# Delta rule chunks: the diagonal blocks of sixteen rows inverted by substitution on GpSimd through a DRAM scratch

## The chip, the core and the metric

The kernel runs on one core of one Trainium2 chip. The metric is the device time of one execution in microseconds (us). The engines are named as in the profile: PE is TensorE's matmul side, PEld its weight loads, DVE is VectorE, ACT is ScalarE, POOL is GpSimd, SP is the queue of SyncE, which here only starts DMAs and waits on semaphores.

## The reference, cut to what matters

The model is two layers over 2 x 1024 tokens of width 128: a gated delta rule, a stack of six local attention layers, a windowed attention and a mixture. The change touches the first only. Per head (2 sequences, 6 heads, key width 128, value width 32) it is a recurrence over the tokens:

```
S = S * exp(g_t)                      # S: 128 x 32
delta = (v_t - k_t S) * b_t
S = S + k_t (outer) delta ;  o_t = q_t S
```

The kernel doesn't step through the tokens. It takes chunks of 128 tokens: inside a chunk the deltas solve a triangular system (I + A) delta = rhs, where A is the strictly triangular 128 x 128 matrix of key products weighted by decay and b. So each chunk of each head needs the inverse of I + A (kept as `inv`) and its transpose (`invT`), and then only a few matmuls carry the state from chunk to chunk.

## The kernel before, in words

`delta_chunks` (L410 to L884) handles 16 units in turn: unit m is chunk m // 2 of sequence m % 2, all six heads at once, in two halves of three heads (a = 0, 1).

For a unit m the work is:

- `sums` (L822, POOL) and `decays` (L532, L534, PE), `decay_factors` (L695, ACT, an exp) and `gains` (L826, POOL) make the weights `gt`.
- `products` (L544, PE) multiplies keys with keys and queries, two heads at a time, into the one PSUM bank `g_ps`; `weigh` (L758, DVE) multiplies by `gt` into `amt`, which holds A transposed and the query part.
- `level` (L837, POOL) masks `amt` with the pattern of level l into `atm[l % 3]`. Level l joins diagonal blocks of 2^l rows to blocks of 2^(l+1).
- Level 0 needs no matmul: `first_turned` (L843, POOL), `first_turn` (L553, PE) and `first_inverse` (L763, DVE) write identity minus the masked matrix.
- Each level l = 1 to 6 then does, for both halves, `lower` (L566, for l = 6 L569; PE), `keep_lower` (L679, ACT), `left` (L591, for l = 6 L593; PE) and `change` (L771, for l = 6 L774; DVE). After each level but the last `turn_inverse` (L576, PE) and `keep_turned` (L683, ACT) renew the transpose.
- With the inverse done: `from_state` (L604), `turn_keys` (L521), `solve` (L612), `to_state` (L620, L621) on PE, `residual`, `solution`, `advance` on DVE, `fade_state` (L850) and `gated` (L856) on POOL.

The order on every engine is written out by hand, in a loop over slots s. In slot s unit s is inverted through levels 1 to 6; the recurrence of unit s - 1 and the preparation of unit s + 1 are put between the levels. Every engine works through its own list in order, and semaphores tie the lists together. A three-head step of fp32 matmuls (`lower`, `left`) is six instructions on PE, a three-head turn is three.

SP has three loads at the start of this stage and nothing after them. The stage is followed by `delta_outputs` (L887), after a barrier of all engines.

## Time and profile before

| | us |
|---|---|
| median of 3 runs (lowest, highest) | 3261.16 (3244.03, 3281.86) |
| the profiled execution | 3263.82 |
| its span, first to last instruction | 3262.1 |
| mean granted TensorE clock | 0.876 of full speed |
| PE busy over the span | 2885.2 (88%) |
| POOL busy over the span | 1830.5 (56%) |

The delta chunks take the stretch from about 195 us to 807 us of the span. What comes before is the projections and convolutions, what comes after is `delta_outputs`, then the local layers from about 880 us. In the profile a row of a stretch or of a group of instructions gives busy time and a count; busy time is not a wait, and PE's busy time has modelled ends. "[idle before <- releaser]" is how long an engine stood and what ended it.

### The profile page before, as it was taken

How to read it: one execution, taken by the hardware profiler on the slowest of the kernel's cores; microseconds unless marked ns; L12 is line 12 of the kernel's file. 1: busy time of each engine (PE TensorE's matmuls, PEld its weight loads, DVE VectorE, ACT ScalarE, POOL GpSimd, SP SyncE). 2: the span in 40 equal slices, each digit the busy share in tenths (PEclk: the TensorE clock that was granted, in tenths of full speed). 3: DMA queues.
4: the chain of work that ended last, by engine and by line, in shares of the span. 5: the costliest groups of instructions: out<-in, count | busy, mean ns of one | idle time of the engine just before them, and what ended most of it. 6: DMA issues, size and time to landing. Idle time of an engine off the chain costs nothing. (4 is left out here: it accounts for less than half of the span.)

```text
span 3262.1 us, 94066 instructions
## 1 busy us (share of the span) xinstructions
PE 2885.2 (88%) x38815; PEld 2010.7 (62%) x38815; DVE 1787.4 (55%) x3522; ACT 1542.9 (47%) x2863; POOL 1830.5 (56%) x2696
## 2 busy tenths in 40 slices
PE   5869999998588999999899999999899976999977
PEld 1259999998356666666566666666666653555444
DVE  5822222222276777776777777776777744434314
ACT  4722222223155656665666655666666641233223
POOL 0044444442188888887878888888878741111111
PEclk9968889887599999999999999999999997577677
DMA  1000000000211121212222121212111110000000
GB/s 29 0 6 1 1 1 1 1 1 17 94 39 49 43 62 41 82 41 64 57 57 63 41 73 50 60 53 74 41 41 48 41 31 13 1 1 1 1 11 14
DMA packets 60625, 109.93 MB, mean 34 GB/s; under 512 B 14366, under 2 KB 18734, under 8 KB 59438
## 3 DMA queue, kind: packets, MB, share of 16 engines
q1 hardware_dynamic: 59280, 102.69, 11.3%
q8 instruction: 310, 5.08, 0.6%
q10 hardware_dynamic: 926, 1.27, 0.1%
q14 instruction: 109, 0.89, 0.1%
HBM read 28.93 MB, written 1.05 MB: 9 GB/s over the span
## 5 line engine op out<-in xcount | busy, mean ns | idle before, releaser
L1681 POOL TENSOR_TENSOR l_rot_a<-l_rot_a,l_rot_b 128x512 f32<-128x512 f32 x384 | 483.8, 1275 | 113.5 <-DVE l_rot_b L1541 112.9
L1169 PE MATMUL l_A<-l_wts,l_H 128*128 128x512 f32 x768 | 416.0, 625 | 27.2 <-ACT l_H L1482 21.3
L1535 DVE TENSOR_TENSOR l_rot_a<-l_A,l_tab 128x512 f32<-128x512 f32 x384 | 265.0, 690 | 289.6 <-ACT l_sq L1401 278.2
L1690 POOL TENSOR_TENSOR l_qk<-l_rot_a,l_rn 128x512 f32<-128x512 f32 x384 | 388.7, 1044 | 21.5 <-POOLq L1728 21.2
L1401 ACT ACTIVATE l_sq<-l_A 128x512 f32<-128x512 f32 x384 | 230.9, 601 | 133.3 <-PE l_A L1169 129.0
L1407 ACT ACTIVATE l_pT<-l_T 128x512 f32<-128x512 f32 x192 | 109.0, 595 | 373.4 <-PE l_T L1215 372.9
L1541 DVE TENSOR_TENSOR l_rot_b<-l_A,l_tab 128x512 f32<-128x512 f32 x384 | 261.5, 681 | 0.0
L1545 DVE TENSOR_REDUCE l_ss<-l_sq 128x8 f32<-128x512 f32 x384 | 259.6, 676 | 0.0
L2010 ACT ACTIVATE a_pT<-a_t 128x384 f32<-128x384 f32 (+1 forms) x256 | 111.2, 463 | 261.2 <-PE a_t L1908 261.1
L1270 PE MATMUL l_T<-ident,l_qk 128*128 128x128 f32 x1536 | 212.6, 282 | 17.3 <-POOL l_qk L1690 14.6
L1270 PEld LDWEIGHTS l_T<-ident,l_qk 128*128 128x128 f32 x1536 | 177.8, 144 | 80.7 <-issue 54.9
L1908 PE MATMUL a_t<-a_qT,a_kT 32*128 32x384 f32 (+1 forms) x512 | 198.0, 651 | 28.3 <-ACT a_pT L2010 28.3
L1753 POOL TENSOR_TENSOR l_pn<-l_sd,l_rs 128x1024 f32<-128x1024 f32 x96 | 182.9, 1905 | 67.8 <-DVE l_rs L1563 67.8
L679 ACT ACTIVATE c_u<-c_ups 128x192 f32<-128x192 f32 x192 | 63.5, 330 | 304.6 <-PE c_ups L566 277.5
L771 DVE TENSOR_TENSOR c_inv<-c_inv,c_wps 128x192 f32<-128x192 f32 x160 | 56.7, 355 | 267.1 <-PE c_wps L591 266.6
L837 POOL TENSOR_TENSOR c_atm<-c_amt,c_blocks 128x768 f32<-128x768 f32 x96 | 156.2, 1642 | 81.6 <-DVE c_amt L758 78.4
L1244 PEld LDWEIGHTS l_O<-l_vw,l_pT 64*32 64x32 f32 x9216 | 135.9, 111 | 106.8 <-ACT l_pT L1407 89.3
L2042 DVE CUSTOM_DVE_ANT_0 a_junk<-a_s,a_mask 128x384 f32<-128x384 f32 (+1 forms) x256 | 125.7, 523 | 138.5 <-PE a_s L1897 136.7
L1276 PEld LDWEIGHTS l_T<-l_oT,l_wts 128*128 128x128 f32 x1536 | 186.4, 192 | 23.3 <-issue 11.3
L2107 POOL TENSOR_SCALAR_AFFINE_SELECT a_pT<-a_pT 128x512 f32<-128x512 f32 x56 | 35.7, 637 | 278.5 <-ACT a_pT L2010 278.5
L1276 PE MATMUL l_T<-l_oT,l_wts 128*128 128x128 f32 x1536 | 187.2, 275 | 0.7 <-ACT l_oT L1425 0.7
L1178 PE MATMUL l_O<-l_wts,l_H 128*128 128x512 f32 x384 | 183.9, 602 | 0.9 <-ACT l_oS L1418 0.5
(340 smaller groups left out, 6635.2 us busy)
## 6 DMA issues: line engine op xcount, KB each, us to landing
l_vw<-l_vn SPq DMA_DIRECT2D x384, 128.0 KB
l_vw<-l_vn SPq DMA_DIRECT2D x360, 64.0 KB
l_wts<-in_l_wts SPq DMA_DIRECT2D x18, 650.0 KB, 4.2
l_tab<-in_l_tables SPq DMA_DIRECT2D x6, 1024.0 KB, 5.2
l_wts<-in_l_wts SPq DMA_DIRECT2D x6, 635.5 KB, 4.1
result<-x SPq DMA_DIRECT2D x4, 256.0 KB, 2.3
d_w_qkv<-in_d_w_qkv SPq DMA_DIRECT2D x1, 864.0 KB
l_scales<-in_l_scales SPq DMA_DIRECT2D x6, 128.0 KB, 5.5
```

Of the source, the lines that this page charges most:

```text
L1169: pe.matmul(A[j % 2][:], cols(m), w_of(m)[:, C_QKV + 512 * j:C_QKV + 512 * j + 512], start=True, stop=True).then_inc(pq_done, 1)
L1178: pe.matmul(O[e][:], cols(m), w_of(m)[:, C_V + 512 * e:C_V + 512 * e + 512], start=True, stop=True).then_inc(v_done, 1)
L1270: last = pe.transpose(T[c % 2][:, P * i:P * i + P], qk[:, c, P * i:P * i + P], ident[:])
L1276: last = pe.matmul(T[0][:, 0:P], w_of(m)[:, C_WO + D * two:C_WO + D * two + D], oT[:, two, :], start=(two == 0), stop=(two == HP - 1))
L1401: act.activation(sq[:, j % 2, :], A[j % 2][:], ACT.Square).then_inc(sq_rdy, 1)
L1535: dve.tensor_tensor(rot_a[p][:, j, :].rearrange("p (a d) -> p a d", d=DH), src.rearrange("p (a d) -> p a d", d=DH), table[:, a, t:t + 1, : ...
L1541: dve.tensor_tensor(rot_b[:, j, :].rearrange("p (a e d) -> p a e d", a=8, e=2), swapped, sins.to_broadcast([P, 8, 2, DH // 2]), ALU.mult). ...
L1545: dve.tensor_reduce(ss[p][:, 8 * j:8 * j + 8], sq[:, j % 2, :].rearrange("p (a d) -> p a d", d=DH), AX, ALU.add).then_inc(ss_rdy, 1)
L1681: pool.tensor_tensor(rot_a[m % 2][:, j, :], rot_a[m % 2][:, j, :], rot_b[:, j, :], ALU.add).then_inc(rot_rdy, 1)
L1690: pool.tensor_tensor(qk[:, j, :].rearrange("p (a d) -> p a d", d=DH), rot_a[p][:, j, :].rearrange("p (a d) -> p a d", d=DH), rn[p][:, 8 * ...
L1753: pool.tensor_tensor(pn[:].rearrange("p a e k -> p e a k"), sd[m % 2][:].rearrange("p (e a) k -> p e a k", e=2), rs[:].rearrange("p (e a o ...
L1908: pe.matmul(t_ps[h % 2][:, c0:c1], kT[r, j, P * t:P * t + P], qT[r, j, around(t)], start=True, stop=True)\
```

## The change

Levels 0 to 3 of the doubling go. In their place the eight diagonal blocks of 16 x 16 of each of the six heads, 48 blocks in all, are inverted by forward substitution on POOL, with one block to a partition. The blocks get to that layout and back by way of DRAM: `amt` is written out in rows, the diagonal blocks are read into `bm` (48 partitions), the inverses `bx` are written back to the diagonal of a zeroed scratch matrix, and that matrix is read as `inv`. All four DMAs of a unit are issued on SP, each one waited for before the next that depends on it. Levels 4, 5 and 6 stay as they were. The transpose that level 4 needs is now a `turn_inverse(s, 3)` on PE. `amt` has three buffers in place of two. The slot order is rewritten: the decays are made two units ahead (slot s does unit s + 2), the products and the block inverse one unit ahead, and the loop has one more slot, starting at s = -2.

The core of the diff:

```diff
+FIRST, LAST = 4, LEVELS - 1
+BLK = 1 << FIRST
+PROBS = GH * P // BLK
...
-        blocks = sb("c_blocks", [P, LEVELS, P], BF16)
+        blocks = sb("c_blocks", [P, LAST - FIRST, P], BF16)
-        amt = [sb(f"c_amt{i}", [P, GH, 2, P]) for i in range(2)]
-        atm = [sb(f"c_atm{i}", [P, GH, P]) for i in range(3)]
+        amt = [sb(f"c_amt{i}", [P, GH, 2, P]) for i in range(3)]
+        atm = [sb(f"c_atm{i}", [P, GH, P]) for i in range(LAST - FIRST)]
+        eye = sb("c_eye", [PROBS, BLK, BLK])
+        bm = sb("c_bm", [PROBS, BLK, BLK])
+        bx = sb("c_bx", [PROBS, BLK, BLK])
+        bt = sb("c_bt", [PROBS, BLK, BLK])
+        lower_out = [nc.dram_tensor(f"c_lower_out{i}", (GH, P + 1, P), F32).ap() for i in range(2)]
+        first_in = [nc.dram_tensor(f"c_first_in{i}", (GH, P + 1, P), F32).ap() for i in range(2)]
...
+        def rows_of(matrix):
+            return bass.AP(tensor=matrix.tensor, offset=0, ap=[[P, P], [(P + 1) * P, GH], [1, P]])
+        def diagonal_of(matrix):
+            return bass.AP(tensor=matrix.tensor, offset=0, ap=[[BLK * (P + 1), PROBS], [P, BLK], [1, BLK]])
...
         def _(sp):
+            sp.wait_ge(cleared, 1)
+            for i in range(2):
+                sp.dma_start(rows_of(first_in[i]), inv[0][:]).then_inc(xo_done, 16)
+            sp.wait_ge(xo_done, 32)
+            for m in range(UNITS):
+                sp.wait_ge(amt_rdy, PAIRS * m + PAIRS)
+                if m >= 2:
+                    sp.wait_ge(bm_ld, 16 * (m - 1))
+                sp.dma_start(rows_of(lower_out[m % 2]), amt[m % 3][:, :, 0, :]).then_inc(ao_done, 16)
+                sp.wait_ge(ao_done, 16 * (m + 1))
+                if m >= 1:
+                    sp.wait_ge(bx_rdy, m)
+                sp.dma_start(bm[:], diagonal_of(lower_out[m % 2])).then_inc(bm_ld, 16)
+                sp.wait_ge(bx_rdy, m + 1)
+                if m >= 2:
+                    sp.wait_ge(inv_ld, 16 * (m - 1))
+                sp.dma_start(diagonal_of(first_in[m % 2]), bx[:]).then_inc(xo_done, 16)
+                sp.wait_ge(xo_done, 32 + 16 * (m + 1))
+                if m >= 2:
+                    sp.wait_ge(u_done, at_level(m - 2, LAST, 1))
+                    sp.wait_ge(tt_done, at_turn(m - 2, LAST - 1, 1))
+                sp.dma_start(inv[m % 2][:], rows_of(first_in[m % 2])).then_inc(inv_ld, 16)
...
             def decays(m, a):
                 pe.wait_ge(m1_rdy, m + 1)
                 if a == 1:
                     pe.wait_ge(gt_rdy, 2 * m + 1)
+                elif m >= 1:
+                    pe.wait_ge(amt_rdy, PAIRS * m)
...
             def turn_inverse(m, l, a):
-                pe.wait_ge(t_rdy, at_turn(m, l, a))
+                if l < FIRST:
+                    pe.wait_ge(inv_ld, 16 * (m + 1))
+                else:
+                    pe.wait_ge(t_rdy, at_change(m, l, a))
...
+            for s in range(-2, UNITS + 1):            # PE
+                for p in range(PAIRS):
+                    if has(s + 1):
+                        products(s + 1, p)
+                    if has(s - 1):
+                        from_state(s - 1, p)
+                if has(s + 2):
+                    decays(s + 2, 0)
+                for a in range(2):
+                    if has(s):
+                        turn_inverse(s, FIRST - 1, a)
+                if has(s + 2):
+                    decays(s + 2, 1)
+                for a in range(2):
+                    if has(s):
+                        lower(s, FIRST, a)
+                    if has(s - 1):
+                        turn_keys(s - 1, a)
+                for a in range(2):
+                    if has(s):
+                        left(s, FIRST, a)
+                    if has(s - 1):
+                        solve(s - 1, a)
...
+            for s in range(-2, UNITS + 1):            # ACT
+                if has(s + 2):
+                    decay_factors(s + 2, 0)
+                for a in range(2):
+                    if has(s):
+                        keep_turned(s, FIRST - 1, a)
+                if has(s + 2):
+                    decay_factors(s + 2, 1)
...
+            for s in range(-2, UNITS + 1):            # DVE
+                for p in range(PAIRS):
+                    if has(s + 1):
+                        weigh(s + 1, p)
+                if has(s - 1):
+                    residual(s - 1)
...
+            def block_inverse(m, lo, hi):
+                def step(ins, k):
+                    ins.then_inc(bx_step, 1)
+                    pool.wait_ge(bx_step, (2 * BLK - 1) * m + k)
+                if lo == 0:
+                    pool.wait_ge(bm_ld, 16 * (m + 1))
+                    if m >= 1:
+                        pool.wait_ge(xo_done, 32 + 16 * m)
+                    step(pool.tensor_copy(bx[:], eye[:]), 1)
+                for j in range(lo, hi):
+                    n, w = BLK - 1 - j, j + 1
+                    factor = bm[:, j, j + 1:BLK].rearrange("p (i o) -> p i o", o=1).to_broadcast([PROBS, n, w])
+                    step(pool.tensor_tensor(bt[:, 0:n, 0:w], factor, bx[:, j:j + 1, 0:w].to_broadcast([PROBS, n, w]), ALU.mult), 2 * j + 2)
+                    last = pool.tensor_tensor(bx[:, j + 1:BLK, 0:w], bx[:, j + 1:BLK, 0:w], bt[:, 0:n, 0:w], ALU.subtract)
+                    step(last, 2 * j + 3)
+                if hi == BLK - 1:
+                    pool.sem_inc(bx_rdy, 1)
...
+            for s in range(-2, UNITS + 1):            # POOL
+                if has(s - 1):
+                    fade_state(s - 1)
+                if has(s + 2):
+                    gains(s + 2)
+                if has(s + 3):
+                    sums(s + 3)
+                if has(s + 1):
+                    block_inverse(s + 1, 0, BLK - 1)
+                for l in range(FIRST, LAST):
+                    if has(s + 1):
+                        level(s + 1, l)
+                if has(s - 1):
+                    gated(s - 1)
```

## Rows read from the trace of the kernel before

**Rows 1.** The page's first part: busy time, share of the span, instructions.

```profile
PE 2885.2 (88%) x38815; PEld 2010.7 (62%) x38815; DVE 1787.4 (55%) x3522; ACT 1542.9 (47%) x2863; POOL 1830.5 (56%) x2696
```

**Rows 2.** Busy time by stretch: length, PE, PEld, DVE, ACT, POOL, granted clock, DMA.

```profile
270.00:774.00 504.00, 500.41 (x3642) 466.58 (x3641) 138.06 (x398) 148.35 (x356) 213.51 (x152) 0.86 0.00 1
```

**Rows 3.** One line's instructions, L826: shortest/median/longest ns, first and last start.

```profile
L826 POOL TENSOR_TENSOR c_gt<-c_gt,c_gain x16: 1469/1470/1472, 202.0 to 743.5; 128x768 f32<-128x768 f32 x16
```

**Rows 4.** Groups of weight loads by line, 270 to 774 us: busy, mean ns, idle.

```profile
L566 PEld LDWEIGHTS c_ups<-c_inv,c_atm 128*128 128x128 f32 x818 | 122.5, 221 | 5.1
L591 PEld LDWEIGHTS c_wps<-c_u,c_invT 128*128 128x128 f32 x826 | 119.4, 212 | 10.2 <-issue 4.6
L576 PEld LDWEIGHTS c_tps<-ident,c_inv 128*128 128x128 f32 x411 | 56.7, 177 | 1.9
```

**Rows 5.** Busy time by stretch, two stretches at the two clock levels.

```profile
413.00:434.00 21.00, 20.77 (x177) 19.38 (x175) 6.34 (x15) 6.55 (x17) 13.35 (x9) 0.99 0.01 2
433.00:447.00 14.00, 14.00 (x66) 12.97 (x66) 2.38 (x10) 3.45 (x8) 3.00 (x3) 0.52 0.00 0
```

**Rows 6.** PE and ACT in order of time: start, length, instruction, idle before.

```profile
196.69 1.49 PE L534 MATMUL c_gps<-c_m,c_tri 128*128 128x384 f32 x2
...
406.76 0.37 PEld L576 LDWEIGHTS c_tps<-ident,c_inv 128*128 128x128 f32 x3
...
407.37 0.81 PE L534 MATMUL c_gps<-c_m,c_tri 128*128 128x384 f32 x2
...
408.21 0.49 ACT L695 ACTIVATE c_gt<-c_gps 128x384 f32<-128x384 f32 x1 [0.32 <-PE c_gps L534]
...
443.45 0.66 PEld L576 LDWEIGHTS c_tps<-ident,c_inv 128*128 128x128 f32 x3
```

**Rows 7.** POOL in order of time, chained small operations of `rsqrt`.

```profile
20.31 0.22 POOL L71 TENSOR_TENSOR n_tmp<-n_tmp,n_mv 128x16 f32<-128x16 f32 x1 [0.18 <-POOL n_tmp L70]
...
173.36 0.59 POOL L71 TENSOR_TENSOR d_rs_tmp<-d_rs_tmp,d_ssq 128x192 f32<-128x192 f32 x1 [0.18 <-POOL d_rs_tmp L70]
```

**Rows 8.** Single lines' instructions on POOL: shortest/median/longest ns.

```profile
L71 POOL TENSOR_TENSOR m_etm<-m_etm,m_ess x3: 181/181/183, 3184.6 to 3187.6; 16x1 f32<-16x1 f32 x3
L1703 POOL COPY l_kT<-l_kT x36: 394/398/402, 941.7 to 2620.3; 128x256 f32<-128x256 f32 x36
L66 POOL TENSOR_SCALAR d_ssq<-d_ssq x1: 858/858/858, 170.2 to 170.2; 128x192 f32<-128x192 f32 x1
```

**Rows 9.** DMA issues: count, KB each, median us from issue to landing.

```profile
result<-x SPq DMA_DIRECT2D x4, 256.0 KB, 2.3
a_mask<-in_a_mask SPq DMA_DIRECT2D x1, 192.0 KB, 2.6
ident<-in_ident SPq DMA_DIRECT2D x1, 64.0 KB, 5.6
x<-in_x SPq DMA_DIRECT2D x1, 0.5 KB, 6.2
m_bcol<-in_m_bcol SPq DMA_DIRECT2D x1, 2.5 KB, 2.5
```

**Rows 10.** Groups of POOL by line, 270 to 774 us.

```profile
L837 POOL TENSOR_TENSOR c_atm<-c_amt,c_blocks 128x768 f32<-128x768 f32 x84 | 136.7, 1642 | 71.0 <-DVE c_amt L758 67.8 <-PE c_ups L566 3.2
L822 POOL TENSOR_TENSOR c_m<-c_tri,logdecay 128x768 f32<-128x768 f32 x13 | 19.1, 1471 | 0.0
L856 POOL TENSOR_TENSOR gate<-x,gate 128x192 f32<-128x192 f32 x14 | 8.3, 591 | 44.2 <-PE c_ups L566 31.9 <-DVE x L743 12.3
L850 POOL TENSOR_TENSOR c_state<-c_state,decay 128x192 f32<-128x192 f32 x14 | 7.1, 509 | 37.5 <-PE c_sps L604 37.5
```

**Rows 11.** In order of time: first unit's last `weigh`, last unit's `left`, last `gated`.

```profile
209.25 0.69 DVE L758 TENSOR_TENSOR c_amt<-c_gps,c_gt 128x512 f32<-128x512 f32 x1 [2.17 <-PE c_gps L544]
...
790.64 0.53 PE L593 MATMUL c_wps<-c_invT,c_u 64*64 64x64 f32 x6 [0.18 <-ACT c_invT L683]
...
806.90 0.59 POOL L856 TENSOR_TENSOR gate<-x,gate 128x192 f32<-128x192 f32 x1 [10.77 <-DVE x L743]
```

More of the change, by code:

```diff
@@ L537, in products @@
             def products(m, p):
-                if p == 0:
-                    pe.wait_ge(gt_rdy, 2 * m + 2)
+                if p == 0 and m >= 1:
+                    pe.wait_ge(bv_rdy, m)
+                elif p == 0:
+                    pe.wait_ge(gt_rdy, 2)
                 else:
@@ L620, in to_state @@
                     pe.matmul(s_ps[:, VD + HV * h:VD + HV * h + HV], kn[:, h, :], xd[:, h, :], start=True, stop=True, skip_group_check=True)
-                    mm = pe.matmul(s_ps[:, HV * h:HV * h + HV], amt[m % 2][:, h, 1, :], xs[:, h, :], start=True, stop=True,
+                    mm = pe.matmul(s_ps[:, HV * h:HV * h + HV], amt[m % 3][:, h, 1, :], xs[:, h, :], start=True, stop=True,
                                    skip_group_check=True)
                 mm.then_inc(od_done, 1)
-            def behind_lower(s, l, a):
-                if l == 1 and has(s - 1):
-                    from_state(s - 1, a)
-                if l == 2 and a == 0 and has(s - 1):
-                    turn_keys(s - 1, 1)
-                if l == 2 and a == 1 and has(s + 1):
-                    decays(s + 1, 0)
-                if l == 3 and a == 0 and has(s + 1):
-                    decays(s + 1, 1)
-                if l == 4 and a == 0 and has(s - 1):
-                    to_state(s - 1, 2)
-                if l == 4 and a == 1 and has(s + 1):
-                    products(s + 1, 0)
-                if l == 5 and a == 0 and has(s + 1):
-                    products(s + 1, 2)
-                if l == LAST and a == 1 and has(s + 1):
-                    first_turn(s + 1, 0)
@@ L643, in behind_left @@
-            def behind_left(s, l, a):
-                if l == 1 and a == 0 and has(s - 1):
-                    from_state(s - 1, 2)
-                if l == 1 and a == 0 and has(s + 1):
-                    turn_values(s + 1)
-                if l == 1 and a == 1 and has(s - 1):
-                    turn_keys(s - 1, 0)
-                if l == 2 and has(s - 1):
-                    solve(s - 1, a)
-                if l == 3 and has(s - 1):
-                    to_state(s - 1, a)
-                if l == 4 and a == 0 and has(s + 1):
-                    products(s + 1, 1)
-                if l == LAST and a == 0 and has(s + 1):
-                    first_turn(s + 1, 1)
@@ L659, in _ @@
-            pe.wait_ge(const_ld, 48)
-            pe.wait_ge(init, 1)
-            for s in range(-1, UNITS + 1):
-                for l in range(1, LEVELS):
-                    for a in range(2):
-                        if has(s):
-                            lower(s, l, a)
-                            if l >= 2:
-                                turn_inverse(s, l - 1, a)
-                        behind_lower(s, l, a)
-                    for a in range(2):
-                        if has(s):
-                            left(s, l, a)
-                        behind_left(s, l, a)
+            pe.wait_ge(const_ld, 64)
@@ new lines, in _ @@
+            pe.wait_ge(init, 1)
+            for s in range(-2, UNITS + 1):
[23 more added lines that the diff above has]
+                    if has(s):
+                        lower(s, FIRST + 1, a)
+                        turn_inverse(s, FIRST, a)
+                    if has(s - 1):
+                        to_state(s - 1, a)
+                for a in range(2):
+                    if has(s):
+                        left(s, FIRST + 1, a)
+                    if a == 0 and has(s - 1):
+                        to_state(s - 1, 2)
+                if has(s + 1):
+                    turn_values(s + 1)
+                for a in range(2):
+                    if has(s):
+                        lower(s, LAST, a)
+                        turn_inverse(s, FIRST + 1, a)
+                for a in range(2):
+                    if has(s):
+                        left(s, LAST, a)
```

175 lines of the change are left out of this document (67 added, 108 removed).

## The prediction

> **What bounds the kernel now.** I began with the page's busy shares: PE is the busiest engine over the whole span, POOL second among the others [rows 1]. A share over the whole span says little about one stage, so next the stretches. Between 270 and 774 us, fourteen units of the delta chunks, PE is busy 500 of 504 us and the weight loads alone 467, while POOL has 214, ACT 148, DVE 138 and DMA nothing [rows 2]. PE's modelled ends could flatter it, but the weight loads at 93% can't hide a wait for a chain: PE is truly full, and what leaves its list is time. The period of a unit is read from an instruction that occurs once in each: L826 starts at 202.0 the first time and 743.5 the sixteenth, 541.5 / 15 = 36.1 us [rows 3]. The stretch shows no DMA, so SP is free.
>
> By the code a unit has 266 instructions on PE: 72 for `lower`, 72 for `left`, 36 in the turns with `first_turn`, and 86 for the rest (2 + 6 + 6 + 12 + 24 + 12 + 24). The trace has 3642 in 504 us, 261 a unit; a few records are missing. The groups of levels dominate the loads [rows 4]. The clock moves between its two levels, 2.4 and 1.2 GHz: 177 instructions take 21 us at 0.99 (0.119 each), 66 take 14 us at 0.52 (0.212 each), and the stage as a whole has 0.86 [rows 2, 5].
>
> **PE's part.** Levels 1, 2 and 3 take away 6 `lower` and 6 `left` steps of 6 instructions and 3 turns of two halves with 3 each (turns 1 and 2 and the first turn; the turn of level 3 stays): 72 + 18 = 90 of 266, 34%. Read from the loads instead: 0.6 x (122.5 + 119.4) + 0.4 x 56.7 = 168 of 467, 36% even without the first turn [rows 2, 4]. So PE needs 176 / 266 x 36.1 = 23.9 us a unit at the clock of before. At the head of a slot products and `weigh` alternate on one bank, with `from_state` as cover; about 1 us for that and the two shortened last levels. PE's own bound: 25 us.
>
> **The new wait and its circle.** `turn_inverse(s, 3)` on PE now waits for the load of `inv`. Behind it in PE's list stand `decays(s + 2, 1)`, level 4 and the whole recurrence of unit s - 1. That decay feeds the exp on ACT, this feeds `gains(s + 2)` on POOL, and behind `gains` and `sums` in POOL's list stands the block inverse of unit s + 1, whose result makes the next load of `inv`. This is a closed circle once per slot, and I price it piece by piece.
>
> *Turn, decay, exp.* At the full clock a turn, its decay and the exp run from 406.76 to 408.70, 1.94 us, and the second turn adds 0.37: 2.3. At the low clock the turns are 0.66 each and the decay's fp32 matmuls 1.49 instead of 0.81: 3.6 [rows 6]. PE has just stood waiting there, so I take the upper one, 3.5.
>
> *Gains and sums.* 1.47 each [rows 3, 10]: 2.9.
>
> *Block inverse.* One copy of 256 elements and 30 dependent operations of n x w elements with n + w = 16. The products sum to 680 over 15 steps, 45 on average. A chained POOL operation of 16 elements takes 0.22, of 192 elements 0.59, each after a gap of 0.18 [rows 7]; the line through them gives 0.283 at 45, so 0.46 with the gap: 13.9, and 0.398 + 0.18 for the copy [rows 8]: 14.5 us. Lower end: 0.18 of work, as at one element, and the gap for all: 11.4. Upper end: each as long as 192 elements, 23.9, for no row has runs of 1 to 15 elements under a broadcast. I stay on the line because few partitions cost nothing extra (16 of them, one element: 0.181 [rows 8]) and `fade_state`, with a broadcast operand and 192 elements, takes 0.509 [rows 10], no more than the plain ones.
>
> *Two DMAs.* `bx` goes out to DRAM: 48 KB in runs of 64 B; the nearest row is the store of 256 KB in runs of 512 B, 2.3 us. The matrix comes in: 384 KB; the nearest row is `a_mask`, 192 KB in 2.6; with another half I take 3.1. With 0.15 before each, 5.7 us. Lower end 4.8 (2.3 and 2.5), upper end the two dearest landings, 5.6 and 6.2, which is 12.1 [rows 9].
>
> Here a rule speaks against the change: the runs of 64 B. The rows bound the store only by one with longer runs. The Trainium skill ("DMA: Bandwidth & Descriptors", the opening table) says that below 512 B the DMA engines read, modify and write and lose line rate. By that the store would take longer, perhaps by as much as it spends on its packets; as an estimate from that page, half a microsecond a unit, 8 us in all. No run here shows it, and the sum goes without it.
>
> Circle: 3.5 + 2.9 + 14.5 + 5.7 = 26.6, with handoffs 27 us. It is longer than PE's 25, so PE waits some 2 us a slot at the turn.
>
> **Not on the path, and what covers it.** The way out (`amt` to DRAM 2.8, blocks in 2.6, from the store and `m_bcol` [rows 9]) runs between `weigh(s + 1)` and the block inverse. SP can only issue it once the load of `inv` for unit s is under way, and then it lands some 3 us after that load; the block inverse starts 6.4 us after it. If PE reaches the head of the slot late this cover goes; then the path over two slots decides: rest of PE's slot 17, head 6, out and in 5.7, block 14.5, back 5.7, which is 49 for two, still under 27 each. POOL's remaining work (two masks 3.3 instead of six and a `first_turned`, `gated` 0.6, `fade_state` 0.5 [rows 10]) lies under the two DMAs; its total is 14.5 + 2.9 + 4.4 = 21.8 of 27. ACT and DVE lose ten and eight operations a unit and wait already. SP's queue carried nothing. The zeroing of the scratch (two stores of 2.3) lies before the first `weigh` ends.
>
> **The sum.** The first unit is weighed at 209.9 as before [rows 11]. The block inverse of unit 0 now stands behind `gains(1)`: two decays and exps at the low clock, some 2.4 each, 4.9, and `gains` and `sums`, 2.9: 217.8. Plus 14.5 and 5.7: `inv` of unit 0 is there at 238. Fifteen periods of 27 lead to 643. Slot 15 after its turn has 176 - 39 = 137 instructions less the decays, at 0.136 with a little waiting: 17, so 660. The last recurrence takes what it took, 791.1 to 807.5, 16.4 [rows 11]: 676.5. Before it was 807.5. That is 131 us less. The profiled execution took 3263.8, so 3133; it stands 2.7 above the median of the runs, and I predict 3132.
>
> **Rivals.**
>
> *PE stays the bound.* The block inverse goes at its lower end or the clock stays low; then a period is 25 and the time 3133 - 15 x 2 = 3103. For it: 27 and 25 are close. Against: the circle has four landings and gaps at favourable prices already. Chance 0.18.
>
> *The trips through DRAM are dear.* Upper landings in the circle, 12.1 instead of 5.7: period 33.4, and 3133 + 16 x 6.4 = 3235. For it: the only large load in short rows is x, 6.2. Against: that one moved 1 MB in all and `ident` stood behind it in the queue; the other three rows land in 2.3 to 2.6. Chance 0.10.
>
> *The steps on POOL are dear, and the kernel is slower.* The place is the 30 dependent operations; the price is that of the dearest small POOL operation, 0.858 with 0.19 of gap, 1.05 a step [rows 8]: 31 x 0.59 = 18 us more, period 45, time 3133 + 16 x 18 = 3421. The point from which it decides: 131 / 16 = 8.2 us more, that is 0.73 a step instead of 0.46. For it: shapes that no row has, and every one is on the path. Against: 0.858 was a first use; its successors were at 0.5 to 0.7 for four times the elements. Chance 0.09.
>
> *The clock falls.* PE waits in each slot. At 0.52 an instruction takes 0.212 instead of 0.136 [rows 5]: 176 make 37.3, period 37 and 3133 + 150 = 3283, no change. Against: PE would then be always busy, and with PE always busy the clock of before was 0.86 [rows 2]. The Trainium skill ("TensorE: Matmul & The Clock Gate", on what is happening) says that the low clock is the default and activity lifts it, so a wait each slot would favour this rival; the trace has low spells with PE full too [rows 5], so it neither bears this out nor speaks against it. Chance 0.06.
>
> **Numbers.** The forecast has 0.57. The four rivals make 1 with it. From 3085 (PE's bound with a clock slightly higher than before) to 3235 (dear DRAM trips) lie the forecast and the first two rivals, 0.85. One per cent is 33 us, about what a measurement of this kernel can tell from no change. Faster by more: 0.57 + 0.18 and a part of the dear trips, 0.78. Within: the rest of those and the clock, 0.13. Slower: 0.09.
>
> **What would show it.** POOL's steps should start every 0.4 to 0.55 us and a block inverse last 14 to 15; `gains` should start right after an exp whose decay waited behind the turn; the largest wait of PE should be the turn, released by the DMA of `inv`; L826 should recur every 27 us; the DMAs of a unit should land in 2 to 3.5. I am wrong if the steps take over 0.7, if POOL waits for `bm` and not for the exp, or if the clock of the stage is under 0.7.

## The result and the profile after

| | before | after |
|---|---|---|
| median (lowest, highest) of 4 and 4 runs, us | 3259.72 (3244.03, 3281.86) | 3102.51 (3071.02, 3110.8) |
| the profiled execution, us | 3263.82 | 3103.04 |
| its span, us | 3262.1 | 3101.3 |
| mean granted clock over the span | 0.876 | 0.873 |
| first `gains` to last `gated`, start, us | 202.0 to 806.9 [rows 3, 11] | 201.9 to 649.7 |

The ratio is 0.9495, with a 95% interval of 0.9409 to 0.9582. An execution more than 1.5% above the fastest of its kernel counts as slow and is left out of every ratio here, though not out of the medians. The forecast was 3132 in a range of 3085 to 3235. Of the 161 us between the two profiled executions 157 lie before the end of the delta chunks: their last `gated` comes that much earlier, and from there to the end it is 2455.2 us before and 2451.6 after.

In the code after, `gains` is L860, `sums` L856, the masks `level` L866, the block inverse L879 (copy), L883 (multiply) and L884 (subtract), `turn_inverse` L616, the decays L575 and L577, the exp L731, the products L589, `weigh` L799. The DMAs are L528 (`amt` out), L532 (blocks in), L536 (inverses out) and L541 (`inv` in).

The page after, its first part and two of its DMA rows, against [rows 1]:

```profile
PE 2707.9 (87%) x37375; PEld 1824.3 (59%) x37375; DVE 1738.0 (56%) x3395; ACT 1476.6 (48%) x2703; POOL 1833.4 (59%) x3112
...
c_lower_out<-c_amt SPq DMA_DIRECT2D x16, 384.0 KB, 2.5
c_inv<-c_first_in SPq DMA_DIRECT2D x16, 384.0 KB, 3.4
```

PE has exactly 38815 - 37375 = 1440 instructions less, 90 for each of 16 units. The same stretches as [rows 2, 5] of before, now of the changed kernel (columns as there, with GB/s at the end):

```profile
410.00:433.00 23.00, 22.73 (x179) 20.32 (x178) 6.92 (x21) 6.67 (x16) 15.63 (x37) 1.00 0.18 42
215.00:560.00 345.00, 328.12 (x2256) 287.73 (x2257) 89.65 (x266) 86.89 (x206) 216.59 (x514) 0.85 0.15 36
270.00:590.00 320.00, 317.39 (x2241) 281.90 (x2241) 88.92 (x270) 85.13 (x202) 194.56 (x463) 0.88 0.16 37
```

In the steady part PE is busy 317 of 320 us. The engine that bounded the stage before bounds it still, which the forecast denied. 2241 instructions in 320 us make 25.1 us for a unit of 176, and the period read from `gains` says the same; this is its row, to be laid beside [rows 3]:

```profile
L860 POOL TENSOR_TENSOR c_gt<-c_gt,c_gain x16: 1469/1470/1472, 201.9 to 566.2; 128x768 f32<-128x768 f32 x16
```

The second of the sixteen starts at 214.90, so fourteen periods take 351.3 us, 25.1 each. That mean is made of two kinds of slot: ten take 22.6 to 23.4 us, and four, each with a stretch of some 20 us at the low clock, take 29.6 to 31.4. The waits for the load of `inv`, from the view of the one line L616 (its lengths in ns, then what ended PE's idle time before it, in us, and how often; PE and its weight loads counted apart):

```profile
L616 PE MATMUL c_tps<-ident,c_inv x288: 272/273/476, 234.5 to 631.1; 128*128 128x128 f32 x144
its engine sat idle before it (us, times) until:
  DMA c_inv<-c_first_in: 32.9, 9
```

This is 33 us on the two sides of PE together, 17.2 of it at the first unit. The forecast had a wait of 2 us in every slot. Now one slot at the full clock in order of time (start, length, instruction, idle time before it), read as the circle was priced:

```profile
405.65 0.32 SPq L536 DMA_DIRECT2D c_first_in<-c_bx  x1
...
405.84 1.13 PE L589 MATMUL c_gps<-kqT 128*128 128x256 f32 x4
...
407.63 0.38 SPq L541 DMA_DIRECT2D c_inv<-c_first_in  x1
...
411.84 0.81 PE L577 MATMUL c_gps<-c_m,c_tri 128*128 128x384 f32 x2
...
412.48 0.82 PE L616 MATMUL c_tps<-ident,c_inv 128*128 128x128 f32 x6
...
413.48 0.81 PE L577 MATMUL c_gps<-c_m,c_tri 128*128 128x384 f32 x2
...
414.32 0.49 ACT L731 ACTIVATE c_gt<-c_gps 128x384 f32<-128x384 f32 x1 [0.38 <-PE c_gps L577]
...
414.89 1.47 POOL L860 TENSOR_TENSOR c_gt<-c_gt,c_gain 128x768 f32<-128x768 f32 x1 [2.68 <-ACT c_gt L731]
...
416.32 1.47 POOL L856 TENSOR_TENSOR c_m<-c_tri,logdecay 128x768 f32<-128x768 f32 x1
...
417.73 0.39 POOL L879 COPY c_bx<-c_eye 48x256 f32<-48x256 f32 x1
...
428.36 0.21 POOL L884 TENSOR_TENSOR c_bx<-c_bx,c_bt 48x15 f32<-48x15 f32 x1
...
428.47 1.13 PE L589 MATMUL c_gps<-kqT 128*128 128x256 f32 x4
428.65 0.32 SPq L536 DMA_DIRECT2D c_first_in<-c_bx  x1
...
430.62 0.38 SPq L541 DMA_DIRECT2D c_inv<-c_first_in  x1
...
435.11 0.82 PE L616 MATMUL c_tps<-ident,c_inv 128*128 128x128 f32 x6
```

Everything the forecast drew is there: the exp behind the second decay behind the turn, `gains` right after it, the block inverse behind `sums`, the two DMAs. But the block inverse takes 10.84 us (417.73 to 428.57), not 14.5. The load issued at 407.63 lands 3.4 later, at about 411.0, and PE comes to the turn at about 412.2. The circle at the full clock is 2.3 + 0.1 + 2.9 + 10.85 + 0.1 + 2.0 + 3.4 = 21.7; PE's own list takes 22.6 (L589, 405.84 to 428.47). It is a near miss: the circle has about 1 us of slack. The way out has little too: the blocks are read at 414.11 and land 2.1 later, at 416.2, and the block inverse starts at 417.73.

### The profile page after: what moved, and what is told of

Its sections match the earlier page's. It is cut to its first block and busy times, and to the rows that moved or that the text cites. A ratio compares the mean times of both kernels' runs of the same rounds, so it can differ in the third digit from the quotient of the medians.

```text
span 3101.3 us, 91235 instructions
## 1 busy us (share of the span) xinstructions
PE 2707.9 (87%) x37375; PEld 1824.3 (59%) x37375; DVE 1738.0 (56%) x3395; ACT 1476.6 (48%) x2703; POOL 1833.4 (59%) x3112
## 3 DMA queue, kind: packets, MB, share of 16 engines
q1 hardware_dynamic: 111808, 117.52, 13.8%
## 5 line engine op out<-in xcount | busy, mean ns | idle before, releaser
L1207 PE MATMUL l_A<-l_wts,l_H 128*128 128x512 f32 x768 | 416.1, 626 | 25.5 <-ACT l_H L1520 21.5
L1946 PE MATMUL a_t<-a_qT,a_kT 32*128 32x384 f32 (+1 forms) x512 | 197.9, 650 | 28.3 <-ACT a_pT L2048 28.2
L1314 PEld LDWEIGHTS l_T<-l_oT,l_wts 128*128 128x128 f32 x1536 | 186.3, 192 | 23.5 <-issue 11.3
L1282 PE MATMUL l_O<-l_vw,l_pT 64*32 64x64 f32 x9216 | 156.9, 237 | 13.8 <-issue 11.2
L1207 PEld LDWEIGHTS l_A<-l_wts,l_H 128*128 128x128 f32 x768 | 127.6, 200 | 65.8 <-issue 38.9
L1253 PE MATMUL l_T<-ident,l_pn 128*128 128x128 f32 x768 | 125.0, 301 | 45.3 <-DVE l_H L1607 44.9
```

The source lines that it names most:

```text
L1207: pe.matmul(A[j % 2][:], cols(m), w_of(m)[:, C_QKV + 512 * j:C_QKV + 512 * j + 512], start=True, stop=True).then_inc(pq_done, 1)
L1282: last = pe.matmul(O[e][WIN * wd:WIN * wd + WIN, DH * pair:DH * pair + DH], pT[r, pair, WIN * wd:WIN * wd + WIN], keys, start=True, stop=True,
L1314: last = pe.matmul(T[0][:, 0:P], w_of(m)[:, C_WO + D * two:C_WO + D * two + D], oT[:, two, :], start=(two == 0), stop=(two == HP - 1))
L1946: pe.matmul(t_ps[h % 2][:, c0:c1], kT[r, j, P * t:P * t + P], qT[r, j, around(t)], start=True, stop=True)\
```

## The experiments

Three theories. **P**: PE's list is the bound, the circle is hidden. **C**: the circle is the bound, or so near to it that PE's gain can't be had without it. **K**: PE is the bound, but its time is instructions times the granted clock, and what is done to the stage moves the clock; it was formed only after "less work on PE" had been run. All medians are set against the kernel before on the same chips. In the tables, "last `gains`" and "last `gated`" are start times in the profiled execution and "clock" is the mean from 215 to 560 us.

### The changed kernel again, for comparison

> The changed kernel itself once more, as the common base of the others. Its trace shows a unit every 25.1 us on average (22.6 in stretches at the full clock), PE busy 317 of 320 us, and the circle turn, exp, gains, sums, block inverse, two DMAs at about 21.7 us at the full clock. Theory P (PE is the bound, the circle has about a microsecond of slack): 3100, within 1%. Theory C (the circle sets the period, PE only fills it): the same time; this run tells nothing apart, the next three are read against it.

3074.79 us (3071.45 to 3094.29), ratio 0.945 [0.9416, 0.9484]; last `gains` 555.7, last `gated` 629.9, clock 0.87. The same program as above; the profiled executions differ by 32 us in all and 20 us in the stage. Eleven of its fourteen periods take 22.6 to 23.4 us, three 30.4 to 30.8. The intervals of the two ratios overlap, so below it is this second run that experiments are compared with (by the ratios where the chip is another), and a difference under some 25 us is not read as one.

### No substitution: the circle cut by 10 us

```diff
-                    pool.wait_ge(bx_step, (2 * BLK - 1) * m + k)
+                    pool.wait_ge(bx_step, m + k)
...
-                for j in range(lo, hi):
+                pool.wait_ge(bx_step, m + 1)
+                for j in range(0):
```

The 30 dependent operations are left out, so the identity goes through the scratch in place of the inverses; copy and DMAs stay.

> The 30 dependent POOL operations of each block inverse are left out (the copy of the identity stays, and all four DMAs), so the circle is 10.4 us shorter and PE has the same work. Theory P: only the first unit, before PE has anything to do, gets 10.4 us shorter, and the few waits at the turn go: 10 to 25 us less than the changed kernel, near 3083. Theory C: every period shrinks until PE's own work stops it, so clearly more, 60 us or above.

3079.03 us (3042.47 to 3089.4), ratio 0.9415 [0.9368, 0.9462]. No wait on the load of `inv` is left:

```profile
L616 PE MATMUL c_tps<-ident,c_inv x288: 272/273/473, 224.8 to 616.8; 128*128 128x128 f32 x144
its engine sat idle before it (us, times) until:
  issue: 4.1, 17
```

Taking 30 x 0.35 = 10 us out of each turn of the circle, 160 us of POOL's work, changes nothing in the total that the measurement can tell: the ratio's interval overlaps the changed kernel's. P had 10 to 25 us less, and that isn't shown either. The periods in the profiled executions tell more than the total. From the fourth `gains` on they are the same with and without the substitution, 22.6 to 22.9 us at the full clock and 30.4 to 30.8 in a slot with a low spell. Only at the head of the stage, before PE's list is full, are two of them shorter, 15.1 and 18.2 us for 23.4 and 23.2. The last `gains` starts at 535.0 (555.7 in the changed kernel), but the last `gated` at 635.3 (629.9): from 545.7 on the clock stays low to the end of the stage, and what the head won is lost there. The circle is not the bound, and C in its strong form falls.

### Less work on PE

```diff
-                for k in range(HALF):
+                for k in range(HALF if l == LAST or m == 0 else 1):
```

The same edit stands in `lower` and in `left`. In levels 4 and 5 (from unit 1 on) they compute one head of three: 32 of 176 instructions of a unit go, and part of the computation with them. A second kernel has both edits, this one and the missing substitution.

> In levels 4 and 5 only one head of three is multiplied in lower and left (all three in unit 0), so PE has 32 of 176 instructions less in each unit; POOL, DMAs and the other engines keep theirs. Theory P: the period falls until the circle stops it, from 25.1 to about 22.5 to 23, so 30 to 40 us less than the changed kernel, and PE now waits at the turn for the load of inv in nearly every slot. Theory C: no change, within 8 us.

> Both at once: 32 PE instructions less per unit and the 30 POOL operations left out. Theory P: the circle no longer stops PE, which gives back its whole 32 x 0.14 = 4.5 us a unit, 65 to 70 us, and 10 in the first unit: 75 to 85 us less than the changed kernel. Theory C: the same as without the substitution alone, since then the circle's gain is what counts, with some of PE's added.

| | median us | ratio, 95% | last `gains` | last `gated` | clock |
|---|---|---|---|---|---|
| changed | 3074.79 | 0.945 [0.9416, 0.9484] | 555.7 | 629.9 | 0.87 |
| less PE | 3136.4 | 0.9628 [0.9598, 0.9658] | 596.8 | 679.3 | 0.68 |
| less PE, no substitution | 3121.43 | 0.9567 [0.9537, 0.9597] | 585.0 | 669.9 | 0.68 |

Neither P nor C allows this: less work, and 62 us more time. With the circle cut it is 47 us more, so the circle isn't the reason. (Cutting it gives this kernel some 15 us, and the two ratios' intervals don't overlap; 13 of them are two shorter periods at the head of the stage.) What moved is the clock, from 0.87 to 0.68, with PE still busy nearly all the time. The median turn on PE takes 418 ns instead of 273, and nine of the fourteen periods of the first of the two kernels take 27.4 us. This brought up K; in the prediction a lower clock stood only as a rival tied to waits.

### Is it the clock? PE work added back

```diff
+                for i in range(1 if l == LAST else 1):
+                    pe.matmul(u_ps[a][:, 192:448].rearrange('p (h t) -> p h t', h=2), identb[:], blocks[:], start=True, stop=True, skip_group_check=True)
```

The kernel with less PE work, with matmuls added whose results nobody reads: one of 256 bf16 columns ahead of each half of `lower` and `left` in levels 4, 5 and 6, two of 128 columns for each pair in `to_state` and in `from_state`. In the kernel below it ("wide fillers") the computation is whole, and only the last level's and `to_state`'s ten are added: the line above reads `range(1 if l == LAST else 0)` there.

> The kernel with two heads of three left out of lower and left in levels 4 and 5 (3136 us at a clock of 0.68 in the stage) with fillers: a 256-column bf16 matmul ahead of each half of lower and left in all three levels, two of 128 columns in each to_state and one pair in from_state. PE gets more work than in that kernel. Theory K: the clock of the stage goes back above 0.85 and the time falls by 40 us or more, to 3070 to 3095. Theory W (that kernel was slower through some wait, not the clock): the time stays or goes up by 15.

> Nothing is left out; ten bf16 matmuls per unit are added whose result nobody reads: one of 256 columns ahead of each half of lower and left of the last level, two of 128 columns in each to_state, the narrow stretch of a slot (64 and 32 columns) in which the spells at 1.2 GHz began. They cost PE about 0.8 us a unit at the full clock. Theory K (the time is PE's list at the clock that it is granted, and the narrow stretch loses the clock): the three spells of 20 us between 240 and 600 us go or get short, 25 us back for 13 spent, so 5 to 25 us less than the changed kernel. Theory P without the clock: 13 us more.

The stretch from 240 to 540 us of the kernel with less PE work, then of the same with the fillers, then of the whole computation with ten fillers, then of the changed kernel:

```profile
240.00:540.00 300.00, 286.47 (x1553) 245.16 (x1551) 74.17 (x225) 72.49 (x175) 168.44 (x405) 0.69 0.14 33
```

```profile
240.00:540.00 300.00, 286.31 (x2300) 241.24 (x2299) 94.93 (x288) 89.15 (x220) 213.46 (x512) 0.99 0.18 43
```

```profile
240.00:540.00 300.00, 295.38 (x2332) 259.81 (x2332) 88.02 (x267) 83.87 (x201) 198.70 (x474) 1.00 0.16 39
```

```profile
240.00:540.00 300.00, 294.03 (x2101) 260.83 (x2101) 82.92 (x252) 80.98 (x192) 189.53 (x450) 0.89 0.15 37
```

The first two show K for this kernel. PE is busy the same 286 us in both, but 1553 instructions get through in one and 2300 in the other. The kernel with the added matmuls does strictly more and takes 3040.48 us (3035.54 to 3045.81), ratio 0.9327 [0.9276, 0.9377], against 3136.4: 96 us less, 98 by the ratios, and more than the 40 or so that K had asked for. Its last `gains` starts at 516.8 and its last `gated` at 583.9, instead of 596.8 and 679.3. The Trainium skill ("TensorE: Matmul & The Clock Gate", on what is happening) has activity lift the clock from its low default; these two agree in direction, 0.69 to 0.99, though the busy share of PE is the same in both.

The same kernel measures the circle. With the clock held and PE's list shorter, its turn waits for `inv` again and again:

```profile
L618 PE MATMUL c_tps<-ident,c_inv x288: 272/273/477, 232.2 to 569.0; 128*128 128x128 f32 x144
its engine sat idle before it (us, times) until:
  DMA c_inv<-c_first_in: 32.6, 19
```

Much of the 32.6 us is the first unit's wait, but from the fifth `gains` on every period is 21.5 or 21.6 us. Here the circle is the bound, and it takes what adding up its pieces gave, 21.7.

For the whole computation the fillers do less good: clock 0.97 in the stage, and the mean period is 23.5 us (last `gains` 540.9) where the comparison run has 24.5 (last `gains` 555.7). At the full clock a period is 23.6 instead of 22.6, so the ten fillers cost 1 us a unit. But the median is 3100.41 us (3084.0 to 3123.07), ratio 0.9518 [0.947, 0.9566]. From 581.0 on, where the last units run out, the clock stays low for 109 us, 47 of them inside the stage, and the last `gated` starts at 627.5, only 2 us before that of the comparison run: what the stage won by its middle it lost at its end. The profiled execution, 3084.0 us, is the shortest of the six, so this trace doesn't show what the others spent more. The kernel isn't faster than the changed one.

### Fillers to the end, and in the kernel before

```diff
-                for i in range(1 if l == LAST else 0):
+                for i in range((l == LAST) + (m >= UNITS - 2)):
...
+                for i in range(2 * (m >= UNITS - 3)):
+                    pe.matmul(s_ps[:, 2 * VD:512], identb[:], causal[:], start=True, stop=True, skip_group_check=True)
...
-                for i in range(2):
+                for i in range(2 + 2 * (m >= UNITS - 3)):
```

This is set against "wide fillers". The last units get more of them. The kernel before gets the same ten as "wide fillers".

> Nothing is left out. The ten wide matmuls of before, and in the last three slots, which lack the products and decays of later units, more of them: one of 256 columns ahead of each half of lower and left in every level of units 14 and 15, two more of 128 columns in to_state and two in from_state of units 13 to 15. With the ten alone the stage had the full clock until 581 us and then 1.2 GHz to its end at 627. Theory K (PE's list at the granted clock): the last slots keep the full clock and end some 15 to 20 us earlier, so the last gating at about 610 and 5 to 20 us less than the changed kernel. If the clock falls at the end for another reason, 2 us more than with the ten.

> The kernel of before with the same ten wide matmuls per unit in the last level and in to_state (nothing left out). Its stage had a granted clock of 0.86 and 36.1 us a unit, with a spell at 1.2 GHz in each unit. Theory K: if the fillers hold the clock, a unit takes 36.1 x (1 - 0.14) + 0.8 = 31.9 and the kernel 60 us less; if they miss the stretch where the spells begin (the start of the next slot, levels 1 and 2), the clock stays and it takes 10 us more. In the first case more than a third of what the change brought could have been had without it.

To the end: 3086.2 us (3066.56 to 3099.44), ratio 0.9451 [0.9407, 0.9495], level with the changed kernel's 0.945; K's 5 to 20 us less are not shown. This time spells of the low clock came at 365 and 539 us in the middle of the stage (20.5 us each), and the end had the full clock until 624.5 but for a spell from 601 to 607.5: last `gains` 560.6, last `gated` 636.2, clock 0.91. So the same fillers (up to unit 13 the two kernels are the same) that had 1.00 from 240 to 540 in one execution don't hold it in another; whether fillers can give a gain in the whole computation stays open.

In the kernel before: 3264.48 us (3256.61 to 3288.93), ratio 1.0012 [0.9981, 1.0043]. The stretch of [rows 2], of before with fillers:

```profile
270.00:774.00 504.00, 499.84 (x3699) 462.77 (x3698) 137.12 (x388) 145.21 (x349) 208.80 (x149) 0.87 0.00 1
```

Clock 0.87 for 0.86, about one low spell in each unit as before. The fillers bring nothing where they don't move the clock. Their cost is under what the ratio can tell; in the profiled execution a period is (753.9 - 200.9) / 15 = 36.9 us for 36.1.

### A longer circle

```diff
...
+                    for r in range(2):
+                        step(pool.tensor_tensor(bt[:, 0:n, 0:w], factor, bx[:, j:j + 1, 0:w].to_broadcast([PROBS, n, w]), ALU.mult), 3 * j + 2 + r)
...
```

Each multiply of the substitution is done twice: 15 operations, 5.1 us, more in the circle and none on PE.

> Each multiplication of the block inverse is done twice (15 more dependent POOL operations, 0.34 us each with the gap, 5.1 us a unit); nothing is left out. The circle grows from 21.7 to 26.8 us at the full clock. Theory P (PE's list is the bound at 22.6 at the full clock, the circle has one microsecond of slack): 5 in the first unit, and about 1.5 to 4 in each period, in all 35 to 65 us more than the changed kernel. Theory C (circle sets the period now): 16 x 5.1 = 82 us more. Theory K (what counts is the clock of the stage): PE now waits in every slot, so the clock of the stage falls under 0.8 and the time goes up by more than 82.

3178.65 us (3166.05 to 3187.65), ratio 0.9738 [0.9683, 0.9794]: 104 us more than the changed kernel in its run, 94 by the ratios. Last `gains` 632.9, last `gated` 731.5, clock 0.78, and now PE does stand at the turn:

```profile
L616 PE MATMUL c_tps<-ident,c_inv x288: 272/417/477, 239.4 to 712.9; 128*128 128x128 f32 x144
its engine sat idle before it (us, times) until:
  DMA c_inv<-c_first_in: 117.1, 20
```

The period is (632.9 - 214.8) / 14 = 29.9 us. At the full clock the circle would be 21.7 + 5.1 = 26.8, but eight of the fourteen periods are 28.2 to 28.4, and that is what this circle takes. In the slot shown PE waits 5 us, the granted clock goes to its low level within that wait (324.2 to 331.0), and turn, decay and exp behind it take 3.7 us (327.19 to 330.86) and not 2.3:

```profile
327.19 1.54 PE L616 MATMUL c_tps<-ident,c_inv 128*128 128x128 f32 x6 [5.03 <-DMA c_inv<-c_first_in]
...
330.37 0.49 ACT L731 ACTIVATE c_gt<-c_gps 128x384 f32<-128x384 f32 x1 [1.11 <-PE c_gps L577]
```

The load of `inv` lands in 3.7 us, 0.3 later than in the changed kernel, with the store of `amt` now issued right behind it. The six other periods, 29.2 to 40.2, hold longer low spells. So this is the forecast's mechanism at work, one step to the side of the change, and here its 3.5 for turn and exp behind a wait comes out. The price, 94 to 104 us, is far above 16 x (26.8 - 25.1) = 27 us and above P's 35 to 65. It doesn't tell C's 82 from K's "more than 82", but the clock is under the 0.8 that K named.

### An extra semaphore increment in each step

```diff
...
                     pool.wait_ge(bx_step, (2 * BLK - 1) * m + k)
+                    pool.sem_inc(bx_tick, 1)
```

The steps of `rsqrt` from which the forecast took the gap of 0.18 increment a second semaphore after each operation, with an instruction of its own (`sem_inc`); the substitution doesn't. Here it does.

> Each step of the block inverse adds one to a further semaphore after its wait, as rsqrt does; nothing else changes. The chained operations of rsqrt stood 0.18 us apart, those of the block inverse 0.08. If the extra increment is the difference, the gap goes to 0.18 and the block inverse from 10.8 to 13.9 us; if not, the gap stays at 0.08.

POOL in order of time, the changed kernel, then this one:

```profile
400.07 0.29 POOL L883 TENSOR_TENSOR c_bt<-c_bm,c_bx 48x64 f32<-48x64 f32 x1
400.44 0.31 POOL L884 TENSOR_TENSOR c_bx<-c_bx,c_bt 48x64 f32<-48x64 f32 x1
400.83 0.30 POOL L883 TENSOR_TENSOR c_bt<-c_bm,c_bx 48x63 f32<-48x63 f32 x1
```

```profile
400.20 0.29 POOL L884 TENSOR_TENSOR c_bt<-c_bm,c_bx 48x64 f32<-48x64 f32 x1 [0.18 <-POOL c_bx L885]
400.67 0.31 POOL L885 TENSOR_TENSOR c_bx<-c_bx,c_bt 48x64 f32<-48x64 f32 x1 [0.18 <-POOL c_bt L884]
401.16 0.29 POOL L884 TENSOR_TENSOR c_bt<-c_bm,c_bx 48x63 f32<-48x63 f32 x1 [0.18 <-POOL c_bx L885]
```

The lengths are equal, 0.29 and 0.31. Only the gap differs: 400.07 + 0.29 to 400.44 is 0.08, against 0.18. So the missing 0.10 of each step is this second increment, issued as its own instruction. One execution, 3146.19 us; a block inverse takes 13.8 us (418.31 to 432.10), PE waits at the turn in 22 places (78.3 us on its two sides together), the clock is 0.79 and the last `gated` starts at 692.3, 43 us later than in the first profile of the changed kernel and 62 later than in the second. Ten of the fourteen periods are 24.6 to 26.5 us, above the 22.6 of PE's list: with the gap that the forecast took, the circle is the bound, as it said.

### Dense blocks in DRAM

```diff
-                sp.dma_start(bm[:], diagonal_of(lower_out[m % 2])).then_inc(bm_ld, 16)
+                sp.dma_start(bm[:], bass.AP(tensor=lower_out[m % 2].tensor, offset=0, ap=[[BLK * BLK, PROBS], [BLK, BLK], [1, BLK]])).then_inc(bm_ld, 16)
...
```

`bm` is read and `bx` written as whole blocks of 1 KB in place of 16 runs of 64 B, from and to the head of the scratch; the values are then not those of the diagonal blocks.

> The blocks are stored to and read from one dense piece of DRAM in place of the diagonal of the matrix (same bytes, 1 KB in a row for each partition where it was runs of 64 B with gaps); the values that the levels then use aren't the inverses. In the changed kernel the store lands in 2.0 us and the read in 2.1. If runs of 64 B cost extra, both land earlier, at 1.5 or less; if the landing is all fixed cost, both stay within 0.2.

One execution, 3106.3 us, last `gated` 655.5. The DMAs from 230 to 560 us, of the changed kernel and then of this one (last figure: us from issue to landing):

```profile
c_bm<-c_lower_out SPq DMA_DIRECT2D x13, 48.0 KB, 2.1
c_first_in<-c_bx SPq DMA_DIRECT2D x13, 48.0 KB, 2.0
```

```profile
c_bm<-c_lower_out SPq DMA_DIRECT2D x14, 48.0 KB, 1.7
c_first_in<-c_bx SPq DMA_DIRECT2D x13, 48.0 KB, 1.6
```

The runs of 64 B cost 0.4 us a transfer (0.3 for the read if the comparison run is taken, where it lands in 2.0), between the two outcomes that were expected. The Trainium skill ("DMA: Bandwidth & Descriptors", the opening table) has transfers below 512 B lose line rate, and the trace agrees in direction. It gives no time for it: the half microsecond was the prediction's own estimate, and it came near. The circle isn't the bound in this kernel, so the gain isn't expected at the end; one execution can't show more.

### The transpose by DMA

```diff
+                sp.dma_start(diagonal_of(turned_in[m % 2]), bxT[:]).then_inc(xoT_done, 16)
...
+                sp.dma_start(invT[m % 2][:], rows_of(turned_in[m % 2])).then_inc(invT_ld, 16)
...
+                    pool.tensor_copy(bxT[:], bx[:].rearrange("p i j -> p j i")).then_inc(bxT_rdy, 1)
```

A version that takes more from PE: `invT` at level 3 comes through a second scratch, so six transposes of PE and two copies of ACT go; with the fillers to the end. The computation is whole.

> Nothing is left out. The transpose that level 4 needs is no longer made by PE: POOL copies the blocks transposed, SP stores them to a second scratch and loads invT from it, so PE has 6 instructions and ACT 2 less per unit, and the decays no longer stand behind the load of inv; fillers as in the kernel with fillers to the end. Theory P with the clock held: 0.8 us a unit less than that kernel, 13 us in all. Against it: the two further DMAs share the queue, and the load of invT lands 1 to 2 us after that of inv; if the circle decides, no gain or up to 20 us more.

3075.93 us (3050.85 to 3107.63), ratio 0.9406 [0.9362, 0.945]; last `gains` 534.1, last `gated` 622.5, clock 0.96:

```profile
240.00:540.00 300.00, 294.38 (x2325) 261.15 (x2325) 89.34 (x271) 77.23 (x183) 211.77 (x505) 0.99 0.24 59
```

Its periods are 22.8 to 23.5 us, it has no low spell between 261 and 571 us, and from 571.8 on the clock is low. It is the shortest stage of all whole versions and has the lowest ratio of them, but the interval overlaps the changed kernel's. No version with the whole computation was shown to be faster than the change itself.

## Why the prediction was right or wrong, point by point

**The total** was right in direction and inside the range; 30 us too slow. Its last step is a slip: 3133 less 2.7 is 3130, not 3132. **The mechanism was not the forecast's but its first rival's**, PE stays the bound, with 0.18 of chance and 3103 us; measured 3102.5. The fit of that figure is luck in part, since the changed kernel's own executions go from 3071 to 3111.

**PE's part** held: 90 instructions a unit are gone, to the instruction, and a unit takes 25.1 us where 25 stood, as a mean of slots of 22.6 and of some 30. The reasoning "PE is truly full, what leaves its list is time" gave the result. But it holds only at a given clock, as the kernel with less PE work shows: there PE was just as full, and what left its list was not time.

**The circle** was drawn rightly and priced wrongly, at 27 where it takes 21.7, and 21.5 where it was made the bound. The failed step is the gap in the block inverse:

| term, us | forecast | measured at the full clock |
|---|---|---|
| turn, decay, exp | 3.5 | 2.3 |
| `gains`, `sums` | 2.9 | 2.9 |
| block inverse | 14.5 | 10.84 |
| two DMAs | 5.7 | 2.0 + 3.4, and 0.1 |

The line through the lengths [rows 7] held: 0.283 at 45 elements forecast, 0.26 and 0.28 the medians of L883 and L884. Short runs, the broadcast and 48 partitions cost nothing that shows: 15 elements take 0.21, where the row with 16 had 0.22. The gap of 0.18 came from rows of operations that are followed by a second semaphore increment. The trace of before has chained operations without one as well, in the local layers, and they would have given the right price. POOL in order of time, kernel before:

```profile
917.58 0.26 POOL L1725 TENSOR_TENSOR l_rn_t<-l_rn_t,l_ss 128x36 f32<-128x36 f32 x1
917.93 0.31 POOL L1726 TENSOR_SCALAR l_rn_t<-l_rn_t 128x36 f32<-128x36 f32 x1
918.33 0.26 POOL L1727 TENSOR_TENSOR l_rn<-l_rn_t,l_rn 128x36 f32<-128x36 f32 x1
```

From 917.58 + 0.26 to 917.93 is 0.09. With 0.08 the sum is 30 x (0.283 + 0.08) + 0.48 = 11.4, just where the forecast's lower end was, and the circle 23.9, or 22.7 with the 2.3 of the full clock: under PE's 25. The other term that was too high, 3.5 for turn and exp, rested on "PE has just stood waiting there", which follows from the circle being the bound; it fell with it. Where PE does wait, in the kernel with the longer circle, it is 3.7.

**The DMAs** were near. The load of 384 KB takes 3.4 where 3.1 stood, the store with runs of 64 B 2.0 where 2.3 stood, the way out 2.5 and 2.1 where 2.8 and 2.6 stood. Landings like the two dearest of [rows 9], 5.6 and 6.2, never came (the longest of the four kinds is 4.6, of `inv` 3.9), which takes the dear trips away as a rival. The half microsecond for runs of 64 B, which the sum left out, was 0.4, and the measured 2.0 includes it.

**What was said to lie off the path** did: the way out, POOL's masks, SP's queue. Between 260 and 620 us POOL stood ahead of the block inverse once, for 4.1 us, and not for `bm`. But the way out has 1.5 us of cover in the slot shown, not the 3.4 of the forecast (6.4 less 3), since SP issues `amt` only when `weigh` is done, at 411.56, after the load of `inv` has landed.

**The sum** went: first `inv` at 234.5 (238 forecast), the last unit's first turn at 606.7 (643), fifteen periods of 24.8; the end of the stage at 650.3 (676.5). The last slots took 43.6 us where 17 + 16.4 stood, and they ran at the low clock:

```profile
600.00:650.00 50.00, 44.25 (x228) 42.30 (x228) 7.71 (x30) 6.89 (x16) 6.70 (x12) 0.54 0.04 9
```

So 36 us less up to the last turn and 10 more behind it leave the stage 26 us under the forecast.

**The rivals.** Dear steps on POOL and dear trips through DRAM did not come: 0.35 a step, 2.0 to 3.4 a trip. The clock did not fall in the change, 0.88 in the steady stretch against 0.86, but the rival named the sharpest danger. It was tied to waits of PE and priced only there. The runs show both: behind a wait the clock falls, as in the longer circle, and it falls without one too, 0.69 with PE busy 286 of 300 us. In this kernel the change kept the clock; nothing in the forecast's reasoning would have told that from the case where 32 more instructions were gone and the clock with them.

**Open.** Why the low spells start is not known. Where they start is on record: the four spells of 17 to 20 us in the first profile of the changed kernel (272.9, 371.8, 470.8, 545.9) all begin during the first `lower` of the last level, 1 to 2 us behind the 32-column matmuls of `to_state`. With PE full most spells last 7 to 20 us, but some don't end before the stage does (47 us with the ten fillers, 90 without the substitution), and their number differs between executions of one program. The spread of the changed kernel, 3071 to 3111, is large beside one of them: a slot with a spell takes some 8 us more, 30.8 for 22.6. Whether fillers can hold the clock in the whole computation with a gain was tried three times and not settled.

## What to carry to other kernels

A price for a chain of small dependent operations is lengths plus gaps, and over 30 steps the gap decides: take it from a row whose instructions have the same waits and increments as yours, not only the same engine and size. When a closed circle and a full engine come out within a few per cent of each other, say so as two cases of like chance, since one tenth of a microsecond a step chooses between them. And where TensorE is the bound, "less work" and "less time" are the same only if the granted clock stays: set the clock of the stage beside the instruction count in every comparison.

## What was not expected of the hardware

- With PE busy 286 of 300 us in both, two kernels got a mean granted clock of 0.69 and 0.99, and the one with 747 instructions more in that stretch has a median 96 us shorter. Matmuls that nobody reads made that kernel faster, and did nothing for the kernel before (ratio 1.0012).
- A further semaphore increment behind each chained POOL operation, as an instruction of its own, costs 0.10 us a step, 0.18 of gap instead of 0.08; with 31 of them a unit, in a circle with 1 us of slack, the stage was 43 and 62 us longer in the one execution made than in the two profiles of the changed kernel.
- Runs of 64 B cost a transfer of 48 KB 0.4 us, 2.1 and 2.0 instead of 1.7 and 1.6 in one execution each, and DRAM as a way to re-lay data between partitions costs 2.0 + 3.4 us from the last write to the load's landing.
